# One core, two-layer graph network: where the products of the bias vectors stand, and which engine splits Wv

## The chip, the core and the metric

The kernel runs on one core of one Trainium2 chip. A core has five instruction queues that run side by side and meet only at semaphores: PE (TensorE, matrix products and transposes into PSUM), DVE (VectorE), ACT (ScalarE), POOL (GpSimd) and SP (SyncE, here used to issue DMAs). The metric is the device time of one execution in microseconds; lower is better. Three executions of the kernel before took 311.39 to 311.70 us, median 311.57 us.

## The reference

Node features x (1024 x 512) go through two layers, each on a layer-normed and rectified copy h of x and each added back to x.

```python
def layer_0(h, src, dst):                 # attention over the edges
    q, k, v = h @ Wq + bq, h @ Wk + bk, h @ Wv + bv
    adj = zeros(1024, 1024).at[src, dst].set(1.0)
    a = q @ k.T / sqrt(512)
    a = a * adj + (1.0 - adj) * NEG       # NEG = -1e6
    return softmax(a, axis=-1) @ v

def layer_1(h, src, dst):                 # two rounds of degree-weighted sums over edges plus self loops
    h = agg(h @ W1 + b1)
    h = relu(batch_norm(h) * gamma + beta)
    return agg(h @ W2 + b2)
```

There are 16384 edges, sorted by dst. dst is drawn as 1024 times the square of a uniform number, so low numbers of dst have many more edges than high ones.

## The kernel before, in words

**Products to full precision.** Each f32 operand is split into a rounded part "hi" and the rest "lo", and a product is three matmuls (lines 948 to 950: lo by hi, hi by lo, hi by hi). A tile that PE leaves in PSUM is an *item*: ACT writes its hi (`hi_of`, line 459), then DVE subtracts to get its lo (`lo_of`, line 651). A weight that comes by DMA is split in two loads j = 0, 1 of 128 x 1024 each: before the change ACT copies the hi of Wv (line 414) and DVE makes the lo (line 636).

**Items.** `start` holds 16: the transposes of Wk and Wq (`t`, eight), M = Wq Wk^T in four blocks (`m`), and the transposes of the first four row blocks of h (`h`). `ahead[i]` holds what PE makes ahead of count group i: v = h Wv by row blocks, the other four h, q = h M in quarters, and `w`.

**Count groups.** The edge counts are built in 16 groups of 64 dst each, in the order 14, 15, 0, 1, 2, ... (`ORDER`). For each group DVE writes one-hot tiles chunk by chunk (a chunk is 128 edges): `src_oh` at line 668, one instruction a chunk, and `dst_oh` at line 670, one instruction for a round of two chunks (the first round) or three. PE multiplies them (line 1018), and ends a group with a small matmul (line 1032). A ring of four rounds (`RING`) lies between DVE and PE: DVE can be four rounds ahead. The third group in this order, group 2, is dst 0 to 63, the one with the most edges. The bounds of a group's chunks are read at run time into registers (`bounds_of`, line 660 on DVE).

**Order on DVE, written out by hand.** Early items 0 to 5; one-hots of groups 0 and 1 with items 6 and 7 between; the two lo of Wv (`split_w(0, 0)`, `split_w(0, 1)`); items 8 to 15 (the four `m`, the four `h`); bounds of group 2; then for i = 2 to 15 the lo of `ahead[i - 2]`, the bounds of the next group and the one-hots of group i. After groups 6, 7, 8 and 9 stand the products of the bias vectors with columns of Wk and Wq:

```python
if 6 <= i <= 9:
    columns_of_biases(K if i < 8 else Q, (0, 1) if i % 2 == 0 else (2, 3))
```

Each call multiplies two 128 x 512 blocks by a broadcast bias row and sums along the row into a column of `uw` (line 689); the last call adds bq by bk (line 693). That is nine instructions. Their results are needed by the hi of `q`, from ahead of group 10, and by `w`.

**Order on ACT.** hi of items 0 to 7, `stats(0)` (sums and squares of x blocks 0 and 1), hi of item 8, `split_w(0, (0,))`, `stats(2)`, hi of item 9, `split_w(0, (1,))`, `layer_norm(0..3)` (line 434), hi of items 10 to 15, then the count groups.

**Order on POOL.** Constants; `targets_of(0..2)` (line 355: dst shifted by the group's first, one 128 x 132 instruction a group, which that group's one-hots wait for); `ln1(0)` and `ln1(2)` (lines 349, 314, 351: three small instructions that give the layer norm's factors for x blocks 0, 1 and 2, 3; they wait for the squares from `stats`, and `layer_norm` waits for them); `targets_of(3..7)`, `ln1(4)`, `ln1(6)`, `targets_of(8..15)`.

**Order on PE.** Items 0 to 9, counts of group 0, items 10 and 11, counts of group 1, items 12 to 15 (transposes of h blocks 0 to 3), then for each further group the items of `ahead[i]` and its counts. v block 0 waits for both lo of Wv.

**Order on SP.** Edges, Wq, x blocks 0 to 3, Wv (`load_w(0)`, line 252), x blocks 4 to 7 (each waits for a `layer_norm`, since the four buffers are reused), the bias rows bq and bk into the two places of `bias_row` (line 263, each 2 KB read into 128 partitions), gamma and beta, and more.

Of the kernel before, what the change touches and what calls it, by code (L numbers as in the profile page):

```python
# [17 lines left out]
P = 128  # L18
N = 1024
D = 512  # L20
# [24 lines left out]
ALU = mybir.AluOpType  # L45
ACT = mybir.ActivationFunctionType
AX = mybir.AxisListType
F32 = mybir.dt.float32
# [7 lines left out]
def gnn_kernel(nc, x, src, dst, Wq, bq, Wk, bk, Wv, bv, W1, b1, gamma, beta, W2, b2, out):  # L56
# [61 lines left out]
    bias_row = sb("bias_row", [P, 2, D], F32)  # L118
# [48 lines left out]
    S = {n: ctx.enter_context(nc.semaphore(n)) for n in sem_names}  # L167
# [3 lines left out]
    K, Q = 0, 1  # L171
# [40 lines left out]
    def weight_load(i, j, what):  # L212

        k = KC // LOADS
        w, raw = weights[i][1:3]
        at, part = {"hi": (w, 0), "lo": (w, 1), "raw": (raw, 1)}[what]
        return at[:, part, j * k:(j + 1) * k, :]
# [7 lines left out]
    @block.sync  # L225
    def _(sp):

        sp.dma_start(edge_i[:, 0, :], dst.rearrange("(c j) -> c j", j=P)).then_inc(S["dst_in"], 16)
        sp.dma_start(edge_i[:, 1, :], src.rearrange("(c j) -> c j", j=P)).then_inc(S["src_in"], 16)

        def load_x(n):
            if XT <= n < NT + XT:
                sp.wait_ge(S["h_ready"], n - XT + 1)
            if n >= NT + XT:
                sp.wait_ge(S["x1_ready"], n - NT - XT + 1)
            sp.dma_start(xt[:, n % XT, :], x[(n % NT) * P:(n % NT + 1) * P, :]).then_inc(S[f"x_in{n % XT}"], 16)

        def turn_counts(t):

            if t == 0:  # L240
                sp.wait_ge(S["c16"], 2 * NW)
            if t >= ADJ:
                sp.wait_ge(S["masked"], t - ADJ + 1)
            sp.dma_start_transpose(adj[:, t % ADJ, :].rearrange("p (b n) -> p b n", b=NT),
                                   cnt16[:, t, :, :].rearrange("p b n -> p (b n)")).then_inc(
                S[f"adj_in{t % ADJ}"], 16)

        def load_w(i):

            k = KC // LOADS  # L250
            for j in range(LOADS):
                sp.dma_start(weight_load(i, j, "raw"), weights[i][0].rearrange("(k p) n -> p k n", p=P)[
                    :, j * k:(j + 1) * k, :]).then_inc(S[f"{weights[i][3]}{j}"], 16)

        for j in range(LOADS):
            sp.dma_start(half_of_qk(Q, j), half_in_dram(Wq, j)).then_inc(S[f"Wq_in{j}"], 16)
        for t in range(XT):
            load_x(t)
        load_w(0)
        for t in range(XT, NT):  # L260
            load_x(t)
        for i, b in ((K, bq), (Q, bk)):
            sp.dma_start(bias_row[:, i, :], b.rearrange("(o n) -> o n", o=1).to_broadcast([P, D])).then_inc(S["qk_bias_in"], 16)
        for i, b in enumerate((gamma, beta)):
            sp.dma_start(bcol[:, i, :], b.rearrange("(c p) -> p c", p=P),
                         allow_slow_non_contiguous=True).then_inc(S["bcol_in"], 16)
        for t in range(XT):
            load_x(NT + t)
        sp.wait_ge(S["item_ps"], nth(("v", NT - 1, 0)))
        load_w(1)  # L270
        sp.wait_ge(S["uw_ready"], 4)
        sp.dma_start(bias_row[:, 0, :], bv.rearrange("(o n) -> o n", o=1).to_broadcast([P, D])).then_inc(S["bias_in"], 16)
        sp.dma_start(bias_row[:, 1, :], b1.rearrange("(o n) -> o n", o=1).to_broadcast([P, D])).then_inc(S["b1_in"], 16)
        def turn_p(t, part, split, done, landed):

            sp.wait_ge(S[split], t + 1)
            if t >= 1:
                sp.wait_ge(S[done], t)
            sp.dma_start_transpose(p16T[:, part, :, :], p16[:, part, :]).then_inc(S[landed], 16)

        def turn_h2(t, part, split, done, landed):

            sp.wait_ge(S[split], t + 1)
            if t >= 1:
                sp.wait_ge(S[done], t)
            sp.dma_start_transpose(h16T[:, part, :, :], h16[:, part, :]).then_inc(S[landed], 16)

        for t in range(ADJ):
            turn_counts(t)
        for t in range(NT + 1):  # L290
            if t < NT:
                turn_p(t, 0, "p16_hi", "p_hi", "p16_hi_in")
                turn_p(t, 1, "p16_lo", "p_lo", "p16_lo_in")
            if XT <= t + 3 < NT:
                load_x(NT + t + 3)
            if t == 0:
                load_w(2)
            if t + ADJ < NT:
                turn_counts(t + ADJ)
            if t >= 1:  # L300
                turn_h2(t - 1, 0, "h16_hi", "h2T_hi", "h16_hi_in")
                turn_h2(t - 1, 1, "h16_lo", "h2T_lo", "h16_lo_in")
        sp.wait_ge(S["xb_ready"], NT)
        sp.dma_start(bias_row[:, 0, :], b2.rearrange("(o n) -> o n", o=1).to_broadcast([P, D])).then_inc(S["bias_in"], 16)
        for t in range(NT):
            sp.wait_ge(S["out_ready"], t + 1)
            sp.dma_start(out[t * P:(t + 1) * P, :], xt[:, t % XT, :]).then_inc(S[f"out_done{t % XT}"], 16)
        for u in range(XT):
            sp.wait_ge(S[f"out_done{u}"], 16 * NT // XT)

    @block.gpsimd
    def _(pool):
# [32 lines left out]
        def ln1(t):  # L345

            p = slice(t, t + 2)
            pool.wait_ge(S["x_squares"], t + 2)
            step(pool.tensor_scalar(lnc[:, 1, p], xsum[:, 1, p], 1.0 / D, EPS, ALU.mult, ALU.add))
            step(pw(lnc[:, 2, p], lnc[:, 1, p], 2))  # L350
            pool.tensor_tensor(lnc[:, 3, p], lnc[:, 0, p], lnc[:, 2, p], ALU.mult).then_inc(S["ln_coef"], 2)

        def targets_of(i):

            pool.tensor_scalar(drel(i), dcol[:, :], float(-WIN * ORDER[i]), 0.0, ALU.add, ALU.add).then_inc(S["drel_ready"], 1)

        pool.wait_ge(S["ecol_ready"], 1)
        pool.wait_ge(S["pad_ready"], 1)
        for i in range(3):
            targets_of(i)  # L360
        ln1(0)
        ln1(2)
        for i in range(3, 8):
            targets_of(i)
        ln1(4)
# [40 lines left out]
    def _(act):  # L406
# [3 lines left out]
        def split_w(i, loads=range(LOADS)):  # L410

            for j in loads:
                act.wait_ge(S[f"{weights[i][3]}{j}"], weights[i][4])
                act.activation(weight_load(i, j, "hi"), weight_load(i, j, "raw"),
                               ACT.Copy).then_inc(S["w_hi"], 1)
# [54 lines left out]
            hi_of(item)  # L470
        stats(0)
        hi_of(("m", 0, 0))
        split_w(0, (0,))
        stats(2)
        hi_of(("m", 1, 0))
        split_w(0, (1,))
        for t in range(KC):
            layer_norm(t)
        for item in list(start)[10:]:
# [114 lines left out]
    def _(dve):  # L594
# [39 lines left out]
        def split_w(i, j):  # L634
            dve.wait_ge(S["w_hi"], w_hi_count(i, j))
            dve.tensor_tensor(weight_load(i, j, "lo"), weight_load(i, j, "raw"),
                              weight_load(i, j, "hi").bitcast(F32), ALU.subtract).then_inc(S["w_lo"], 1)
# [21 lines left out]
        def bounds_of(i):  # L659
            return dve.value_load(lohi[0:1, ORDER[i]:ORDER[i] + 1], min_val=256, max_val=257 * NCH)  # L660
# [23 lines left out]
        def columns_of_biases(n, ks):  # L684

            if (n, ks) == (K, (0, 1)):
                dve.wait_ge(S["qk_bias_in"], 32)
            for k in ks:
                ins = dve.scalar_tensor_tensor(out=qk_raw[:, n, k, :], in0=qk_raw[:, n, k, :], scalar=1.0,
                                               in1=bias_row[:, n, :], op0=ALU.mult, op1=ALU.mult,  # L690
                                               accum_out=uw[:, n, k:k + 1])
            if (n, ks) == (Q, (2, 3)):
                ins = dve.scalar_tensor_tensor(out=bias_row[:, 0, :], in0=bias_row[:, 0, :], scalar=1.0,
                                               in1=bias_row[:, 1, :], op0=ALU.mult, op1=ALU.mult, accum_out=bqbk[:, 0:1])
            ins.then_inc(S["uw_ready"], 1)
# [34 lines left out]
        for item in early[6:8]:  # L730
            lo_of(item)
        onehots(1, bounds[1])
        split_w(0, 0)
        split_w(0, 1)
        for item in early[8:]:
            lo_of(item)
        bounds = bounds_of(2)
        for i in range(2, NW):
            for item in ahead[i - 2]:
                lo_of(item)  # L740
            now = bounds
            if i + 1 < NW:
                bounds = bounds_of(i + 1)
            onehots(i, now)
            if 6 <= i <= 9:
                columns_of_biases(K if i < 8 else Q, (0, 1) if i % 2 == 0 else (2, 3))
        for i in range(NW - 2, NW):
            for item in ahead[i]:
                lo_of(item)
# [480 lines left out]
```

## Time and profile before

| | |
|---|---|
| timed executions | 311.39, 311.57, 311.70 us |
| profiled execution, first to last instruction (span) | 309.8 us |
| median of the timed executions less that span | 1.77 us |
| PE busy | 295.1 us, 95% |
| DVE busy | 210.2 us, 68% |
| ACT busy | 143.6 us, 46% |
| POOL busy | 55.4 us, 18% |
| granted TensorE clock, mean | 0.999 |

The profile lists no time of its own for the profiled execution beside its span; what lies around the span is taken as 1.77 us. A busy time is an average over stages: the change touches the stretch from 4 to about 100 us, where the edge counts are built. A line of the timeline gives the start, the time of a run of like instructions, the engine, the line of the kernel, the operation and, in brackets, how long the engine sat idle before and what ended that. Instructions of one engine can overlap at their ends, so the pace of a run is taken from start to start.

### The profile page before, as it was taken

Reading aid. Unit: us, or ns where it says so; the run is one execution under the profiler, and the core shown is the slowest. Engines: PE = TensorE matmul, PEld = TensorE weight load, DVE = VectorE, ACT = ScalarE, POOL = GpSimd, SP = SyncE. Lnnn points to the kernel's source line nnn. Section 1 sums busy time; section 2 is a strip of 40 time slices with the busy share of each in tenths; the row PEclk is TensorE's granted clock in tenths of the full one; section 3 lists DMA queues with packets and bytes.
Section 4 is the critical chain, followed back from the end, with each engine's and each line's share of the span. In section 5 each row is a group of like instructions: output and inputs, shape, how many; then the busy total and the mean of one; then the engine's idle time right before and its main releaser. Section 6 shows DMA issues by size and latency. Waiting matters only on the chain.

```text
span 309.8 us, 4740 instructions
## 1 busy us (share of the span) xinstructions
PE 295.1 (95%) x1319; PEld 227.4 (73%) x1319; DVE 210.2 (68%) x470; ACT 143.6 (46%) x245; POOL 55.4 (18%) x96
## 2 busy tenths in 40 slices
PE   2999969899999999999999999999999999999995
PEld 2977436565666688888888888888788888888884
DVE  3787999999997747667647575757444288376311
ACT  1799944443445626635465445437632035233000
POOL 5234280000000170032121212203010043100000
PEclk9999999999999999999999999999999999999999
DMA  7707040000420127832834636133203000000221
GB/s 268 291 3 204 1 135 0 3 0 0 150 57 3 33 36 107 200 85 53 136 69 102 135 46 124 36 68 59 44 0 70 1 0 2 0 0 2 101 103 68
DMA packets 42310, 21.65 MB, mean 70 GB/s; under 512 B 35760, under 2 KB 36016, under 8 KB 42288
## 3 DMA queue, kind: packets, MB, share of 16 engines
q1 hardware_dynamic: 41744, 20.33, 26.9%
q10 hardware_dynamic: 544, 1.05, 0.9%
q8 instruction: 11, 0.18, 0.2%
q14 instruction: 11, 0.09, 0.1%
HBM read 10.88 MB, written 2.10 MB: 42 GB/s over the span
## 4 chain that ended last, share of the span: by engine, by line
PE 79%; DVE 10%; issue 4%; DVEq 4%; DMA 1%; ACT 1%; SPq 0%; ACTq 0%
PE ps L948 18%; PE ps L950 18%; PE ps L949 18%; PE ps L1196 9%; PE ps L1119 8%; PE ps L1018 5%; DVE src_oh L668 4%; PE ps L986 2%; DVEq L668 2%; DVE dst_oh L670 2%; DMA edge_i<-src_in 1%; DVE hT L651 1%; DVEq L670 1%; DVEq L660 0%; DVEq L674 0%
## 5 line engine op out<-in xcount | busy, mean ns | idle before, releaser
L668 DVE TENSOR_SCALAR src_oh<-iota,ecol 128x512 f16 x149 | 44.2, 346 | 4.0 <-issue 2.9
L1018 PE MATMUL ps<-src_oh,dst_oh 128*128 x149 | 37.9, 382 | 5.4 <-DVE dst_oh L670 4.6
L1018 PEld LDWEIGHTS ps<-src_oh,dst_oh 128*128 x149 | 14.4, 103 | 25.6 <-issue 16.7
L1119 PE MATMUL ps<-cnt,qh 128*128 128x512 f32 x128 | 30.1, 391 | 0.3 <-ACT cnt L541 0.3
L1196 PE MATMUL ps<-qh,cnt 128*128 128x512 f32 x128 | 29.3, 390 | 0.0
L443 ACT ACTIVATE cnt<-ps 64x512 int16<-64x512 f32 x32 | 18.9, 592 | 20.7 <-PE ps L1032 20.3
L1119 PEld LDWEIGHTS ps<-cnt,qh 128*128 128x128 f32 x128 | 23.9, 188 | 5.6 <-DVE qh L827 0.7
L1196 PEld LDWEIGHTS ps<-qh,cnt 128*128 128x128 f32 x128 | 23.9, 188 | 5.2 <-DVE vb L929 0.3
L950 PE MATMUL ps<-v,pT 128*128 128x512 f32 x64 | 25.0, 390 | 0.0
L948 PE MATMUL ps<-v,pT 128*128 128x512 f32 x64 | 24.9, 390 | 0.0
L949 PE MATMUL ps<-v,pT 128*128 128x512 f32 x64 | 24.9, 390 | 0.0
L948 PE MATMUL ps<-hT,qh 128*128 128x512 f32 x64 | 24.9, 389 | 0.0
L949 PE MATMUL ps<-hT,qh 128*128 128x512 f32 x64 | 24.9, 389 | 0.0
L950 PE MATMUL ps<-hT,qh 128*128 128x512 f32 x64 | 24.9, 389 | 0.0
L382 POOL TENSOR_SCALAR lnb<-bnag 128x1 f32<-128x1 f32 x8 | 8.2, 1028 | 82.2 <-DVE bnag L801 82.2
L941 DVE SCALAR_TENSOR_TENSOR xt<-ps,dinv,x 128x512 f32<-128x512 f32 x8 | 5.7, 747 | 17.1 <-PE ps L1196 17.1
L790 DVE TENSOR_SCALAR pT<-p16T 128x1024 fp32r<-128x1024 f16 x8 | 5.5, 693 | 15.9 <-DMA p16T<-p 15.8
L768 DVE COPY_PREDICATED T<-adj,ps 128x1024 f32<-128x1024 int16 x8 | 10.6, 1322 | 7.8 <-PE ps L950 7.8
L525 ACT ACTIVATE hnT<-h16T 128x512 fp32r<-128x512 f16 x8 | 5.1, 632 | 23.2 <-DMA h16T<-h 23.2
L497 ACT ACTIVATE T<-T,smx 128x1024 f32<-128x1024 f32 x8 | 9.2, 1150 | 13.1 <-DVE smx L773 13.1
L466 ACT ACTIVATE T<-zerob,fill 128x1024 f32<-128x1024 bf16 x8 | 9.1, 1147 | 11.9 <-DVE p L780 11.9
L670 DVE TENSOR_TENSOR dst_oh<-iota_w,drel_first 128x384 f16 (+1 forms) x35 | 14.4, 411 | 0.0
(176 smaller groups left out, 658.8 us busy)
## 6 DMA issues: line engine op xcount, KB each, us to landing
xt<-x_in SPq DMA_DIRECT2D x16, 256.0 KB, 3.3
out<-xt SPq DMA_DIRECT2D x8, 256.0 KB, 2.1
qk_raw<-L_gnn_Wk_in ACTq DMA_DIRECT2D x2, 512.0 KB, 4.9
qk_raw<-L_gnn_Wq_in SPq DMA_DIRECT2D x2, 512.0 KB, 6.7
wB_raw<-L_gnn_Wv_in SPq DMA_DIRECT2D x2, 512.0 KB, 8.9
wB_raw<-L_gnn_W_in SPq DMA_DIRECT2D x2, 512.0 KB, 4.3
w_raw<-L_gnn_W_in SPq DMA_DIRECT2D x2, 512.0 KB, 4.8
bias_row<-L_gnn_b_in SPq DMA_DIRECT2D x2, 256.0 KB, 3.7
```

What stands on the lines that cost most here:

```text
L443: act.activation(cnt16[rows, a * KC:(a + 1) * KC, w // 2, :], ps[a * WIN:(a + 1) * WIN, i % 2, :].rearrange("p (s n) -> p s n", n=P), ACT. ...
L466: act.activation(T[:, t % 2, :], zerob[:, 0:1].to_broadcast([P, N]), ACT.Identity, bias=fill[:, t:t + 1]).then_inc(S["mask_set"], 1)
L497: act.activation(T[:, t % 2, :], T[:, t % 2, :], ACT.Exp, bias=smx[:, 1, t:t + 1], scale=SCALE, accum_out=smx[:, 2, t:t + 1]).then_inc(S[" ...
L668: dve.tensor_scalar(src_oh[:, bass.ds(slot, 1), j, :].rearrange("p a n -> p (a n)"), iota[:, :], ecol[:, bass.ds(c + j, 1)], None, ALU.is_ ...
L670: dve.tensor_tensor(dst_oh[:, bass.ds(slot, 1), :, 0:count].rearrange("p a n u -> p (a n) u"), iota_w[:, :, 0:count], drel(i)[:, bass.ds(c ...
L768: dve.copy_predicated(T[:, t % 2, :], adj[:, t % ADJ, :], ps[:, 2 * (t % 2):2 * (t % 2) + 2, :].rearrange("p a n -> p (a n)")).then_inc(S[ ...
L948: pe.matmul(out_, stat(1), mov(0), start=first, stop=False)
L949: pe.matmul(out_, stat(0), mov(1), start=False, stop=False)
L950: return pe.matmul(out_, stat(0), mov(0), start=False, stop=last)
L1018: m = pe.matmul(ps[:, i % 2, :], dst_oh[:, bass.ds(slot, 1), :, j].rearrange("p a n -> p (a n)"), src_oh[:, bass.ds(slot, 1), j, :].rearra ...
L1119: m = pe.matmul(bank(g), qh[:, d, a, c * P:(c + 1) * P], cnt[:, d, n * HALF:(n + 1) * HALF], start=(d == 0 and a == 1), stop=last)
L1196: m = pe.matmul(bank(t), cnt[:, d, t * P:(t + 1) * P], qh[:, d, a, :], start=(d == 0 and a == 1), stop=last)
```

## The change

SP issues the two bias rows right behind Wv, ahead of the waits for x blocks 4 to 7. The split of Wv goes from ACT and DVE to POOL, between `targets_of` and the layer norm's factors. On DVE the two lo of Wv are gone; the four products of Wk's columns stand between the lo of items 8 and 9, and the five of Wq's columns (with bq by bk) behind the bounds of group 2, ahead of that group's one-hots. Nothing stands behind groups 6 to 9 any more.

```diff
         load_w(0)
+        for i, b in ((K, bq), (Q, bk)):
+            sp.dma_start(bias_row[:, i, :], b.rearrange("(o n) -> o n", o=1).to_broadcast([P, D])).then_inc(S["qk_bias_in"], 16)
         for t in range(XT, NT):
             load_x(t)
-        for i, b in ((K, bq), (Q, bk)):
-            sp.dma_start(bias_row[:, i, :], b.rearrange("(o n) -> o n", o=1).to_broadcast([P, D])).then_inc(S["qk_bias_in"], 16)
...
+        def wv_hi(j):
+
+            pool.wait_ge(S[f"wB_in{j}"], 16)
+            pool.tensor_copy(weight_load(0, j, "hi"), weight_load(0, j, "raw")).then_inc(S["w_hi"], 1)
+
+        def wv_lo(j):
+
+            pool.wait_ge(S["w_hi"], w_hi_count(0, j))
+            pool.tensor_tensor(weight_load(0, j, "lo"), weight_load(0, j, "raw"),
+                               weight_load(0, j, "hi").bitcast(F32), ALU.subtract).then_inc(S["w_lo"], 1)
+
         for i in range(3):
             targets_of(i)
+        wv_hi(0)
         ln1(0)
+        wv_hi(1)
+        wv_lo(0)
         ln1(2)
+        wv_lo(1)
         for i in range(3, 8):
             targets_of(i)
...
         stats(0)
         hi_of(("m", 0, 0))
-        split_w(0, (0,))
         stats(2)
         hi_of(("m", 1, 0))
-        split_w(0, (1,))
...
         onehots(1, bounds[1])
-        split_w(0, 0)
-        split_w(0, 1)
-        for item in early[8:]:
+        lo_of(early[8])
+        columns_of_biases(K, (0, 1))
+        columns_of_biases(K, (2, 3))
+        for item in early[9:]:
             lo_of(item)
         bounds = bounds_of(2)
+        columns_of_biases(Q, (0, 1))
+        columns_of_biases(Q, (2, 3))
         for i in range(2, NW):
             for item in ahead[i - 2]:
                 lo_of(item)
...
             onehots(i, now)
-            if 6 <= i <= 9:
-                columns_of_biases(K if i < 8 else Q, (0, 1) if i % 2 == 0 else (2, 3))
```

## Rows read from the trace of the kernel before

**Rows 1.** Busy time by stretch: length, then us busy of each engine, clock, DMA
```profile
18.40:26.40 8.00, 8.00 (x39) 5.70 (x39) 5.67 (x12) 7.88 (x17) 4.65 (x8) 1.00 0.22 62
...
30.80:45.90 15.10, 12.09 (x51) 5.96 (x50) 15.03 (x51) 10.81 (x28) 8.21 (x14) 1.00 0.23 70
```

**Rows 2.** PE's waits from 33 to 46 us: us in total, times, longest
```profile
PE ps L1018 <- DVE dst_oh L670: 2.8, 7, 0.5
```

**Rows 3.** The chain that ended last, 26 to 31.5 us: start, us, what
```profile
26.89 0.61 ACT hT L459
...
27.52 2.06 DVE hT L651 x4
...
29.68 0.31 DVEq L660
...
30.03 0.20 DVEq L660
...
30.79 0.12 DVE src_oh L668
```

**Rows 4.** Timeline of PE, start of count group 2; groups 6, 7, 8 and 10
```profile
33.86 2.56 PE L1018 MATMUL ps<-src_oh,dst_oh 128*128 x11
...
65.91 1.91 PE L1018 MATMUL ps<-src_oh,dst_oh 128*128 x8
67.65 0.18 PE L1032 MATMUL ps<-zerob 128*128 128x32 bf16 x1
...
70.52 1.28 PE L1018 MATMUL ps<-src_oh,dst_oh 128*128 x5
...
72.77 0.18 PE L1032 MATMUL ps<-zerob 128*128 128x32 bf16 x1
...
75.63 2.15 PE L1018 MATMUL ps<-src_oh,dst_oh 128*128 x8
77.62 0.18 PE L1032 MATMUL ps<-zerob 128*128 128x32 bf16 x1
...
85.52 0.61 PE L1018 MATMUL ps<-src_oh,dst_oh 128*128 x2
...
86.97 0.18 PE L1032 MATMUL ps<-zerob 128*128 128x32 bf16 x1
```

**Rows 5.** Timeline of DVE, the three products behind group 9
```profile
81.55 0.67 DVE L689 SCALAR_TENSOR_TENSOR qk_raw<-qk_raw,bias_row 128x512 f32<-128x512 f32 x1
...
83.39 0.67 DVE L651 TENSOR_TENSOR v<-ps,v 128x512 fp32r<-128x512 f32 x1
```

**Rows 6.** Timeline of all engines, 16 to 26 us
```profile
16.94 0.19 POOL L349 TENSOR_SCALAR lnc<-xsum 128x2 f32<-128x2 f32 x1 [4.81 <-ACT T L428]
...
18.09 0.20 POOL L351 TENSOR_TENSOR lnc<-lnc 128x2 f32<-128x2 f32 x1
...
20.10 1.22 DVE L636 TENSOR_TENSOR wB<-wB_raw,wB 128x1024 fp32r<-128x1024 f32 x1
...
22.69 2.92 ACT L434 ACTIVATE T<-xt,lnc 128x512 f32<-128x512 f32 x4
...
22.82 1.28 DVE L636 TENSOR_TENSOR wB<-wB_raw,wB 128x1024 fp32r<-128x1024 f32 x1 [1.50 <-ACT wB L414]
...
25.52 1.06 ACT L459 ACTIVATE M<-ps 128x512 fp32r<-128x512 f32 x2
```

**Rows 7.** DMA issues of the page: KB each, us to landing
```profile
wB_raw<-L_gnn_Wv_in SPq DMA_DIRECT2D x2, 512.0 KB, 8.9
...
bias_row<-L_gnn_bk_in SPq DMA_DIRECT2D x1, 256.0 KB, 4.7
```

**Rows 8.** POOL's groups by line and shape: busy, mean ns
```profile
L378 POOL TENSOR_TENSOR xt<-xt,bias_row 128x512 f32<-128x512 f32 x8 | 10.2, 1293 | 10.7 <-DMA xt<-x_in 10.7
...
L335 POOL CAST identb<-ident 128x128 bf16<-128x128 f32 x1 | 0.3, 291 | 0.0
```

**Rows 9.** Line 355 on POOL, 22 to 27 us: ns min/median/max
```profile
L355 POOL TENSOR_SCALAR drel_first<-dcol x5: 650/656/1250, 22.7 to 25.9; 128x132 f16<-128x132 f16 x5
```

## The prediction

> **What bounds the kernel now.** The page's shares (table above) say only that PE leads and that DVE may bind in places. So I cut the stretch that the edit touches into stages. In count group 2, from 30.8 to 45.9 us, DVE is busy 15.03 of 15.10 us and PE 12.09 [rows 1]; PE's waits there are for `dst_oh`, 2.8 us in seven pieces [rows 2]. So in this group DVE's one-hots set the pace, and whatever delays their start delays the end of the group by as much: the reader should see that DVE has no idle time to absorb anything. Ahead of it, from 18.4 to 26.4, it is the other way round: PE is busy 8.00 of 8.00 us and DVE 5.67 [rows 1]. Between the two lies a handover that the chain of waits spells out: ACT's hi of h block 0 from 26.89, the four lo of h on DVE from 27.52, two register loads, and the first one-hot at 30.79 [rows 3]. From group 6 on PE leads again: its eight chunks take 67.65 - 65.91 = 1.74 us without a wait [rows 4].
>
> **The change, part by part.**
>
> *Products of Wk's columns, four, moved from groups 6 and 7 to 20 us.* Three products take 83.39 - 81.55 = 1.84 us, start to start, so 0.613 us each [rows 5]; four are 2.45 us. The two lo of Wv that leave the same place took 1.22 and 1.28 us with an idle gap of 1.50 between them [rows 6], 4.0 us. DVE is free of one-hots at 20.10; lo of item 8 (0.6) and the four products end near 23.2, item 9 near 23.8. Items 10 and 11 can't come before ACT's hi of them, which started at 25.52 [rows 6]. Cost: nothing, with about 2 us of cover. The bias rows must have landed by 20.7: Wv took 8.9 us from an issue near 5 us, so to about 14, and a bias row took 4.7 us [rows 7]; even one behind the other that is 19. Cost nothing; without this cover DVE would stand until they land, at most as long as they are late.
>
> *Products of Wq's columns, five, moved from groups 8 and 9 to the handover.* 5 x 0.613 = 3.07 us, on the path: they stand behind the lo of h block 3 and ahead of the first one-hot of the group in which DVE sets the pace. They hide something. At the same pace DVE ended the four lo near 27.52 + 4 x 0.613 = 29.97 and started the one-hot at 30.79: 0.81 us in which only registers were loaded and worked out [rows 3]. The first load (29.68 to 29.99) now lies ahead of the products and under the last lo; the second and the arithmetic behind it (30.03 to 30.79) come behind the products, and the queue can begin them while the last product runs, as it began the first load before the last lo had ended. How much is left bare no row shows: between 0 and 0.81. I take 0.4, the middle: the nearest row is the first load, which was covered, but it is a third of this work. Delay of the first one-hot: 3.07 + 0.4 - 0.81 = 2.66 us, from 2.26 to 3.07. Group 2 then ends as much later, and PE and everything behind it with it; the next groups' one-hots and v blocks keep their distances.
>
> *What comes back.* From group 6 on PE leads and DVE's lateness shows only as stretched count groups. Eight chunks unhindered: 1.74 us. Group 7: 72.77 - 70.52 = 2.25, so 0.51 lost. Group 8: 77.62 - 75.63 = 1.99, 0.25 lost; group 9 has the same form (80.54 to 82.56), 0.28 lost. Group 10 has five chunks, 1.09 by the same pace, and took 86.97 - 85.52 = 1.45: 0.36 lost [rows 4]. These are the groups behind the calls in question, and each call is 1.2 to 1.8 us of DVE; without them DVE is ahead by more than these losses. Back: 0.51 + 0.25 + 0.28 + 0.36 = 1.40 us; bounds 0 (PE finds another wait) and 1.40.
>
> *Wv's split on POOL.* ACT loses two copies; that only lets `stats(2)` end near 20.2. POOL's work is new, and no row shows it at this size. The lo (two inputs, 1024 columns) by the row of 512 columns, 1.29 us, less a fixed 0.19 (line 349, two columns): 0.19 + 2 x 1.10 = 2.4 us; twice the whole row is 2.6 [rows 6, 8]. The hi copy by the cast of 128 columns, 0.29: 0.19 + 8 x 0.10 = 1.0 us as I take it, 2.3 if eight times the whole row; the far end, the 128 x 132 f16 row of 0.65 scaled, is 5.0 [rows 8, 9]. What waits behind: `ln1(2)`, and behind that on ACT layer norms 2 and 3, the hi of items 10 and 11, and the hi of h block 0, which is in the chain. wv_hi(0) runs from about 14 to 15, ahead of `ln1(0)` at 16.94, which ends at 18.29 [rows 6]. Then wv_hi(1) to 19.4. Then wv_lo(0): 1.3 us of it are done by 20.7, when DVE starts Wk's products. Beside a DVE instruction that reads two SBUF operands POOL slows: one `targets_of` took 1.25 us beside line 636 on DVE, against 0.65, and DVE's own 1.28 against 1.22 [rows 6, 9]. At that pace of 0.52 the last 1.1 us take 2.1, to 22.9. `ln1(2)` takes 1.35, as `ln1(0)` did (16.94 to 18.29), with a little drag, to 24.4. Layer norms 2 and 3 end at 24.4 + 2 x 0.73 = 25.9, items 10 and 11 at 26.9, h block 0 at 27.5. That is where it ended before (26.89 + 0.61). So the POOL path has used up its slack to the last tenth, and every excess is passed on. I add 0.2 us; bounds 0 and, with the copy at 2.3 us, 1.2; with the far end of 5.0, about 3.8. wv_lo(1) ends near 27, ahead of v block 0, which can't start before the lo of h block 0 (from 27.52 [rows 3]).
>
> The Trainium skill (SBUF — State Buffer, "Who interferes with whom") has a rule against this: a DVE instruction with two SBUF inputs and a GpSimd instruction that reads SBUF exclude each other, and the second to issue blocks fully until the first ends. The row above bears out POOL's loss (0.60 us) but not a loss for DVE (0.06 us). By the rule the sum would be that of the second rival.
>
> *Moves at no cost.* `targets_of(3..7)` starts near 27 instead of 22.73; group 3 needs them after 45. x blocks 4 to 7 are loaded a little earlier. SP issues two DMAs more ahead of waits of many us.
>
> **Sum.** 2.66 + 0.2 - 1.40 = +1.46 us on the span of 309.8 us, so 311.3. The profiled execution has no other time of its own; with the 1.77 us around the span that the median of 311.57 implies, the median should become 313.0 us.
>
> **Rivals.**
>
> *The group's start hides the products.* PE enters group 2 only after v blocks 0 and 1, at 33.86 [rows 4], 3 us after DVE began its first one-hot; with four rounds of ring, DVE's delay could vanish if PE were the later of the two at the end of the group. Then only the give-back is left: -1.40 us, 310.2. It decides the case if PE does not wait for one-hots late in group 2. Against it: the seven waits, up to 0.5 us, and DVE busy for 15.03 of 15.10 us. For it: nothing but the start of the group. The sign also turns wherever the delay falls below 1.40.
>
> *The shared port locks.* wv_lo(0) and Wk's products exclude each other. If POOL holds first, the products run from 22 to 24.5, `ln1(2)`'s steps each wait for one of them, and h block 0 is about 1.2 us late. If DVE holds first, wv_lo(0) starts at 23.2: 25.6 its end, 27.0 `ln1(2)`, 28.4 the layer norms, 30.1 the hi of h block 0, 2.6 late. Sum 2.66 - 1.40 + 1.2 to 2.6 = +2.5 to +3.9: 314.0 to 315.4, say 314.6. For it: the doubled `targets_of`. Against: DVE's 0.06.
>
> *Nothing comes back.* PE's losses in groups 7 to 10 stay, from some handshake rather than DVE's lateness: 2.66 + 0.2 = +2.9, 314.4. Against: group 6, with the same form of handshake, shows no loss.
>
> **Chances.** Forecast 0.63 (its own range 312.3 to 314.0), lock 0.18, nothing back 0.11, hidden 0.08. What this kernel's measurement can tell from no change is 0.2%, 0.62 us. Faster by more: the hidden case less a part of it, 0.07. Within: the rest of that and the forecast's low tail, 0.08. Slower: 0.85. The range, with the low end of the delay below and the POOL bounds and the lock above: 312.0 to 315.0.
>
> **What would show it.** Right: first one-hot of group 2 near 33.6; PE's waits in group 2 as before but about 2.7 us later; groups 7 to 10 at 1.74 and 1.09 us; POOL's lo near 2.4 us, more beside Wk's products; h block 0's hi within half a microsecond of 26.89. Wrong: group 2 ending near 45.9 (products hidden); h block 0 late by over 1 us (lock, or a slow copy); groups 7 to 10 still stretched.

## The result, and the profile after

The changed kernel takes 314.76 us, median of four executions (314.49 to 315.43), against 311.48 us (311.33 to 311.70, four) for the kernel before on the same chip: ratio 1.0111, 95% interval 1.0098 to 1.0124. It is slower by 3.28 us; the forecast was +1.46. The profiled execution took 314.49 us with a span of 312.7 us, 2.9 more than before.

Read first what DVE does ahead of group 2. Its timeline in the kernel after (one-hots now lines 681 and 683, products 702 and 706, lo 664):

```profile
17.37 1.38 DVE L681 TENSOR_SCALAR src_oh<-iota,ecol 128x512 f16 x2
18.67 2.62 DVE L683 TENSOR_TENSOR dst_oh<-iota_w,drel_first 128x256 f16 x1
21.21 0.87 DVE L681 TENSOR_SCALAR src_oh<-iota,ecol 128x512 f16 x3
...
22.34 0.68 DVE L664 TENSOR_TENSOR M<-ps,M 128x512 fp32r<-128x512 f32 x1
22.94 2.45 DVE L702 SCALAR_TENSOR_TENSOR qk_raw<-qk_raw,bias_row 128x512 f32<-128x512 f32 x1
...
25.32 0.77 DVE L702 SCALAR_TENSOR_TENSOR qk_raw<-qk_raw,bias_row 128x512 f32<-128x512 f32 x1
...
27.41 1.88 DVE L664 TENSOR_TENSOR M<-ps,M 128x512 fp32r<-128x512 f32 x3
29.21 2.47 DVE L664 TENSOR_TENSOR hT<-ps,hT 128x512 fp32r<-128x512 f32 x4
31.61 0.68 DVE L702 SCALAR_TENSOR_TENSOR qk_raw<-qk_raw,bias_row 128x512 f32<-128x512 f32 x1
...
34.66 0.61 DVE L681 TENSOR_SCALAR src_oh<-iota,ecol 128x512 f16 x2
```

and POOL's, with its hi (line 362) and lo (line 367) of Wv:

```profile
17.40 1.20 POOL L362 CAST wB<-wB_raw 128x1024 fp32r<-128x1024 f32 x1
18.57 2.44 POOL L367 TENSOR_TENSOR wB<-wB_raw,wB 128x1024 fp32r<-128x1024 f32 x1
...
22.27 0.20 POOL L351 TENSOR_TENSOR lnc<-lnc 128x2 f32<-128x2 f32 x1
22.43 2.41 POOL L367 TENSOR_TENSOR wB<-wB_raw,wB 128x1024 fp32r<-128x1024 f32 x1
24.80 3.93 POOL L355 TENSOR_SCALAR drel_first<-dcol 128x132 f16<-128x132 f16 x5
```

Lay the two side by side. "Alone" means the time that the same instruction takes with POOL idle. A `dst_oh` that takes 0.42 us started 0.10 us behind POOL's first lo and took 2.62: it ended 0.28 us behind that lo. A product, 0.68 us alone, started 0.51 us behind the second lo and took 2.45, to 0.55 us behind its end. The other three products take 0.77 beside `targets_of`, only 0.09 more than alone, and the pair of `src_oh` beside POOL's hi 1.38 instead of 0.61. DVE's account, start to start: group 1's one-hots 17.37 to 22.34, 4.97 us, where the kernel before took 18.12 to 20.10, 1.98; four products 22.94 to 27.41, 4.47 us instead of the 2.45 reckoned. That is 5.0 us lost beside POOL (0.27 of it the 3 x 0.09 beside `targets_of`). Without it DVE's work from group 1 to the lo of h would have been 1.98 + 0.60 + 2.45 + 1.80 (three lo of M) = 6.83 us, and the kernel before took 27.52 - 18.12 = 9.40 [rows 3]: 2.57 us of cover, that is, of idle time which this work, the products included, would leave. 5.01 - 2.57 = 2.44 us stay. The lo of h starts only 1.69 us later, because this execution was 0.75 us ahead by then (17.37 against 18.12).

The stretches that answer to [rows 1], with group 2 now from 34.66 to 49.60:

```profile
18.40:26.40 8.00, 8.00 (x41) 5.91 (x40) 8.00 (x12) 5.59 (x11) 7.69 (x8) 1.00 0.43 133
34.66:49.60 14.94, 11.67 (x48) 5.47 (x47) 14.94 (x53) 7.64 (x19) 7.93 (x14) 1.00 0.22 71
```

In the first one DVE's 5.67 us of 8.00 have become 8.00 (an instruction that is held counts as busy): the idle time that was to hide the products is gone. Group 2 itself is as before, DVE busy throughout, and PE's wait that answers to [rows 2] has 3.1 us in eight pieces:

```profile
PE ps L1032 <- DVE dst_oh L683: 3.1, 8, 0.5
```

The chain of waits, 26 to 35.5 us, no longer goes through ACT's hi of h as in [rows 3] but straight back through DVE's products:

```profile
25.40 2.10 DVE qk_raw L702 x6
27.49 1.80 DVE M L664 x3
```

PE, with the rows that answer to [rows 4] (two idle gaps ahead of v block 0; start and end of group 2; groups 7 and 10):

```profile
28.15 0.66 PE L1000 MATMUL ps<-ident,T 128*128 128x128 f32 x4 [0.85 <-DVE M L664]
29.99 0.47 PE L962 MATMUL ps<-wB,hT 128*128 128x512 f32 x1 [1.18 <-DVE hT L664]
...
37.12 2.87 PE L1032 MATMUL ps<-src_oh,dst_oh 128*128 x11
...
49.57 0.18 PE L1046 MATMUL ps<-zerob 128*128 128x32 bf16 x1
...
74.65 1.91 PE L1032 MATMUL ps<-src_oh,dst_oh 128*128 x8
76.39 0.18 PE L1046 MATMUL ps<-zerob 128*128 128x32 bf16 x1
...
88.47 1.26 PE L1032 MATMUL ps<-src_oh,dst_oh 128*128 x5
89.56 0.18 PE L1046 MATMUL ps<-zerob 128*128 128x32 bf16 x1
```

Group by group PE ends later than before by 3.70 us (group 2: 45.87 to 49.57), 4.15 (group 5: 63.01 to 67.16), 3.62 (group 7), 2.59 (group 10: 86.97 to 89.56) and 2.50 (group 15: 104.11 to 106.61). The rest of the 2.9, about 0.4 us, is added much later, at 250 us, and is taken up below.

### The profile page after: what moved, and what is told of

Same layout as the page of the kernel before. It is cut to its first block, busy times and chain, and to the rows that moved or that the text cites. A ratio compares the mean times of both kernels' runs of the same rounds, so it can differ in the third digit from the quotient of the medians.

```text
span 312.7 us, 4740 instructions
## 1 busy us (share of the span) xinstructions
PE 295.8 (95%) x1319; PEld 227.6 (73%) x1319; DVE 213.2 (68%) x468; ACT 141.8 (45%) x243; POOL 62.2 (20%) x100
## 4 chain that ended last, share of the span: by engine, by line
PE 71%; DVE 16%; issue 5%; DVEq 4%; ACT 2%; DMA 1%; POOL 0%; SPq 0%; ACTq 0%; POOLq 0%
PE ps L962 17%; PE ps L964 17%; PE ps L963 16%; PE ps L1210 9%; PE ps L1133 6%; PE ps L1032 5%; DVE src_oh L681 4%; DVE dst_oh L683 3%; DVEq L681 2%; DVE qk_raw L702 2%; DMA edge_i<-src_in 1%; DVE WT L664 1%; DVE M L664 1%; PE ps L1000 1%; DVE bnst L931 1%
## 5 line engine op out<-in xcount | busy, mean ns | idle before, releaser
L681 DVE TENSOR_SCALAR src_oh<-iota,ecol 128x512 f16 x149 | 45.4, 357 | 6.2 <-PE ps L1032 4.0
L683 DVE TENSOR_TENSOR dst_oh<-iota_w,drel_first 128x384 f16 (+1 forms) x35 | 16.6, 474 | 0.0
L962 PE MATMUL ps<-wB,hT 128*128 128x512 f32 x32 | 13.7, 428 | 1.2 <-DVE hT L664 1.2
```

Source lines behind the costliest of these rows:

```text
L681: dve.tensor_scalar(src_oh[:, bass.ds(slot, 1), j, :].rearrange("p a n -> p (a n)"), iota[:, :], ecol[:, bass.ds(c + j, 1)], None, ALU.is_ ...
L683: dve.tensor_tensor(dst_oh[:, bass.ds(slot, 1), :, 0:count].rearrange("p a n u -> p (a n) u"), iota_w[:, :, 0:count], drel(i)[:, bass.ds(c ...
L962: pe.matmul(out_, stat(1), mov(0), start=first, stop=False)
```

## The experiments

Each is compared with runs of the kernel before on its own chip. Three explanations are weighed here. The lock: POOL's lo and DVE's instruction exclude each other for whole instructions, and that eats the cover of Wk's products. The products: the excess is the products themselves (the bare registers, or nothing given back). The clock: PE ran slowly. A numbered or lettered theory in the text ahead of a run belongs to that run alone.

**One half at a time (e1, e2).** Only POOL's split:

```diff
+        for item in early[8:]:                      # the order of before, without split_w(0, ...)
+            lo_of(item)
...
+            if 6 <= i <= 9:
+                columns_of_biases(K if i < 8 else Q, (0, 1) if i % 2 == 0 else (2, 3))
```

> POOL splits Wv as in the changed kernel; the nine products stay behind groups 6 to 9 as before. Theory 1 (port: a POOL instruction that reads SBUF and a DVE instruction that reads two SBUF operands or runs in a fast mode hold each other up): group 1's one-hots on DVE take about 5 us instead of 2.0, one dst_oh near 2.6 us beside POOL's first lo; DVE still has cover until the lo of h block 0, so the time stays near 311.5 (311.0 to 312.0). Theory 2 (placement: the products' place alone made the loss, POOL is innocent): dst_oh stays at 0.42 us, group 1's one-hots at 2.0 us; time 311.5 too. The instruction times tell them apart, not the total.

311.96 us against 311.61, ratio 1.0013 (1.0003 to 1.0022). The hold is there, on other instructions: the `dst_oh` that was to be held kept its 0.42 us (18.66 to 19.08), and the second `src_oh` of the next round took 2.50 (from 20.05, 0.10 us behind POOL's lo) instead of 0.35. POOL's hi came 0.09 us behind a `src_oh` here, did not hold it, and itself took 1.49 instead of 1.04. DVE:

```profile
19.00 3.81 DVE L681 TENSOR_SCALAR src_oh<-iota,ecol 128x512 f16 x3
...
27.59 2.48 DVE L664 TENSOR_TENSOR hT<-ps,hT 128x512 fp32r<-128x512 f32 x4 [0.18 <-ACT hT L474]
```

and POOL:

```profile
18.49 1.49 POOL L362 CAST wB<-wB_raw 128x1024 fp32r<-128x1024 f32 x1
19.95 2.44 POOL L367 TENSOR_TENSOR wB<-wB_raw,wB 128x1024 fp32r<-128x1024 f32 x1
```

Group 1's one-hots took 4.92 us here too, 2.94 too many, yet the lo of h begins at 27.59 against 27.52: without the products the same cover swallows the hold.

Only the products moved (Wv split by ACT and DVE as before, Wk's products between the two lo of Wv):

```diff
+        lo_of(early[8])
         split_w(0, 0)
+        columns_of_biases(K, (0, 1))
+        columns_of_biases(K, (2, 3))
         split_w(0, 1)
-        for item in early[8:]:
+        for item in early[9:]:
...
+        columns_of_biases(Q, (0, 1))
+        columns_of_biases(Q, (2, 3))
```

> All nine products moved as in the changed kernel, bias rows early, but Wv is split by ACT and DVE as before (on DVE: lo of item 8, first lo of Wv, Wk's products, second lo of Wv). Theory 1: no long one-hot, each product 0.61 us, first lo of h at 27.5 (less about 0.9 if the early part runs ahead as in the changed kernel's profile), the first one-hot of group 2 2.2 us later than before, 1.6 us given back in groups 7 to 10: 312.1 (311.8 to 312.6). Theory 2: the changed kernel's time, 314.5 or more.

312.63 us, ratio 1.0033 (1.0021 to 1.0044), +1.02, just above the expected 311.8 to 312.6. No product is long, the lo of h begins at 27.62, and the first one-hot stands at the end of the last product:

```profile
32.45 0.69 DVE L693 SCALAR_TENSOR_TENSOR bias_row<-bias_row 128x512 f32<-128x512 f32 x1
33.07 0.62 DVE L668 TENSOR_SCALAR src_oh<-iota,ecol 128x512 f16 x2
```

Group 2 ends 2.12 us late, group 10 1.01 us late. So the forecast's sum for the products (2.66 - 1.40 = 1.26) was near. The two halves make 0.35 + 1.02 = 1.4 us apart and 3.28 together: they use one cover twice. That speaks against the products alone, and it is what the lock needs.

**Wq's products back behind groups 8 and 9 (e3)**, the rest as changed:

```diff
-        columns_of_biases(Q, (0, 1))
-        columns_of_biases(Q, (2, 3))
...
+            if 8 <= i <= 9:
+                columns_of_biases(Q, (0, 1) if i == 8 else (2, 3))
```

> The changed kernel, but Wq's products go back behind groups 8 and 9. Theory 1: DVE still loses about 5 us beside POOL, the lo of h start 1.7 us late, the first one-hot of group 2 follows 1.2 us behind the last lo of h; groups 7 and 8 give back, 9 and 10 little: 312.9 (312.3 to 313.4). Theory 2: the delay was Wq's products, so the time falls to 311.0 to 311.6.

313.14 us, ratio 1.0042 (1.0028 to 1.0057). The first one-hot stands at 31.87, 2.79 us earlier than in the changed kernel, but group 2 ends only 0.48 earlier, at 49.09. Between them PE's v blocks 0 and 1 run at half the clock and DVE, its ring full, waits for them. The waits from 30 to 50 us, then the stretches (length, busy times in the order of [rows 1], clock):

```profile
DVE src_oh L681 <- PE ps L1032: 2.2, 1, 2.2
```

```profile
28.00:30.00 2.00, 0.65 (x4) 0.42 (x4) 2.00 (x4) 1.36 (x3) 0.92 (x2) 1.00 0.00 0
...
32.00:34.00 2.00, 2.00 (x7) 1.51 (x6) 2.00 (x8) 1.89 (x7) 0.00 (x0) 0.50 0.00 0
```

So the clock costs time here, as a second consequence of the late lo of h: PE stood 0.69 and 1.19 us, then ran slowly. The ten executions bear it out: five with a mean granted clock of 0.993 to 0.995 took 313.40 to 313.78 us, the five with 0.999 or 1.000 took 311.89 to 312.87. The median of 313.14 lies between the two groups, so that it met the expected range is partly luck. In the changed kernel the same clock (0.50 from 31 to 33 us) shows no price: DVE did not wait there and PE waits for `dst_oh` again from 40 us, and in the two runs of that kernel the four executions with 0.995 took 314.49 to 314.67 us, the four with 0.998 or 1.000 took 314.86 to 315.43.

**POOL's lo in four pieces (e5):**

```diff
+            for a in range(2):
+                for h in range(2):
+                    at = slice(h * D // 2, (h + 1) * D // 2)
+                    ins = pool.tensor_tensor(weight_load(0, j, "lo")[:, a, at], weight_load(0, j, "raw")[:, a, at],
+                                             weight_load(0, j, "hi")[:, a, at].bitcast(F32), ALU.subtract)
+            ins.then_inc(S["w_lo"], 1)
```

> The changed kernel, with each of POOL's two lo instructions cut into four of 128 x 256. Theory 1a (whoever comes first holds the port for its whole instruction): a POOL piece takes about 0.7 us, so no DVE instruction is held up by more than about that: the longest dst_oh 1.2 us instead of 2.62, the longest of Wk's products 1.4 us instead of 2.45; the pieces alternate with DVE's instructions, so DVE's loss in sum stays at 3 to 5 us and the time at 314.0 to 315.0. Theory 1b (the two share a rate): DVE instructions beside POOL all take about twice their time, none over 1.3 us, also in the changed kernel. That kernel's 2.62 already speaks against 1b; the pieces test whether the length of the hold follows the length of POOL's instruction.

313.74 us against 311.70, ratio 1.0071 (1.0055 to 1.0087): 1.24 us of the 3.28 are gone. A DVE instruction is now held for one piece at most, and POOL is held in its turn. DVE's loss is 3.8 us (group 1's one-hots 17.44 to 22.20, the products 22.80 to 26.30) instead of 5.0, within the expected 3 to 5; the time lies below the expected 314.0 to 315.0. DVE:

```profile
18.75 0.95 DVE L687 TENSOR_TENSOR dst_oh<-iota_w,drel_first 128x256 f16 x1
...
22.80 0.68 DVE L706 SCALAR_TENSOR_TENSOR qk_raw<-qk_raw,bias_row 128x512 f32<-128x512 f32 x1
...
24.02 1.22 DVE L706 SCALAR_TENSOR_TENSOR qk_raw<-qk_raw,bias_row 128x512 f32<-128x512 f32 x1
```

POOL's second four pieces took 4.17 us instead of 2.41. The lo of h starts at 28.10 instead of 29.21.

**POOL that only writes (e6)**, a constant by iota in place of its hi, and of its lo likewise, so that this kernel leaves out the split of Wv:

```diff
-            pool.tensor_copy(weight_load(0, j, "hi"), weight_load(0, j, "raw")).then_inc(S["w_hi"], 1)
+            pool.iota(weight_load(0, j, "hi"), pattern=[[0, 2], [0, D]], base=1, channel_multiplier=0,
+                      allow_small_or_imprecise_dtypes=True).then_inc(S["w_hi"], 1)
```

> The changed kernel, with Wv's split left out: POOL writes a constant into the places of hi and lo (iota, 128 x 1024, no SBUF input) instead of reading Wv. Theory A (the read side alone is contended): no product and no dst_oh is held up (0.61 and 0.42 us); src_oh may be. Theory B (any POOL instruction holds DVE up): the DVE instruction that starts beside an iota is held up by about 1 us. Under A the lo of h start at 27.5 and the time is near 312.2 to 312.8, as with the products alone moved; under B 313 to 314.

312.77 us, ratio 1.0036 (1.0021 to 1.0051). Group 10 ends at 87.95, as with the products alone (87.98). DVE, then POOL:

```profile
17.91 1.38 DVE L680 TENSOR_SCALAR src_oh<-iota,ecol 128x512 f16 x2
19.21 0.41 DVE L682 TENSOR_TENSOR dst_oh<-iota_w,drel_first 128x256 f16 x1
19.54 1.34 DVE L680 TENSOR_SCALAR src_oh<-iota,ecol 128x512 f16 x3
...
21.75 0.68 DVE L701 SCALAR_TENSOR_TENSOR qk_raw<-qk_raw,bias_row 128x512 f32<-128x512 f32 x1
```

```profile
18.02 1.13 POOL L362 IOTA wB<- 128x1024 fp32r x1
19.11 1.08 POOL L367 IOTA wB<- 128x1024 fp32r x1
...
21.54 0.99 POOL L367 IOTA wB<- 128x1024 fp32r x1
```

The products and `dst_oh`, with two inputs each, run at full pace beside a POOL instruction that reads nothing (the product at 21.75 lies within the iota that began at 21.54); `src_oh`, with one f16 input, is held all the same. This separates reading from the mere presence of POOL: the part of the loss that hung on the lo's reads is gone. (An iota is also shorter, 1.08 us for 2.44, so the two causes of a smaller loss come together for `src_oh`, not for the products, which were not held at all.)

**The changed kernel once more (e10):**

> The changed kernel once more, on the same chip as e9. If GpSimd's lower half and VectorE's instruction hold each other for their whole length in every execution, a one-hot of destinations takes about 2.6 us and the first product of Wk's rows about 2.4 us again, the lower halves of h begin 1.5 us or more later than the 27.5 us of the kernel before, and the time is 314.4 to 315.2 us. If the hold is a matter of which instruction happens to come first, at least one of the two is short (under 1 us) in this execution, and the time lies 1 us or more below.

314.77 us (314.66 to 315.36) against 311.61, ratio 1.0108 (1.0093 to 1.0124). The same two instructions are held, `dst_oh` 2.61 us and the first product 2.44, and the lo of h starts at 29.16. The two are held in both profiles of this kernel, and in e3's as well (2.61 and 2.44), so it is not a chance meeting.

**Towards a better version (e4, e7, e8, e9).** In e4 Wv is split by ACT and DVE, Wk's products stand between its two lo and Wq's behind groups 7 and 9:

```diff
         split_w(0, 0)
+        columns_of_biases(K, (0, 1))
+        columns_of_biases(K, (2, 3))
         split_w(0, 1)
...
-            if 6 <= i <= 9:
-                columns_of_biases(K if i < 8 else Q, (0, 1) if i % 2 == 0 else (2, 3))
+            if i in (7, 9):
+                columns_of_biases(Q, (0, 1) if i == 7 else (2, 3))
```

> Wv split by ACT and DVE as before; Wk's products stand between the two lo of Wv ahead of group 2, Wq's behind groups 7 and 9. Theory 1: no lock, Wk's products are covered by DVE's idle time before the lo of h, Wq's fit where PE leads: groups 7 to 10 lose 0.3 us or less instead of 1.4; 310.3 (310.0 to 310.9). Theory 2: Wk's products ahead of group 2 are not covered, the lo of h start 1 to 2 us late: 311.5 to 312.5.

310.05 us, ratio 0.9952 (0.9939 to 0.9966). Here Wk's products really are covered (lo of h at 27.27), and the time falls by 1.5 us.

e7 is the same with all `targets_of` ahead of `ln1(4)`:

```diff
-        for i in range(3, 8):
+        for i in range(3, NW):
             targets_of(i)
         ln1(4)
         ln1(6)
-        for i in range(8, NW):
-            targets_of(i)
```

> The kernel with Wk's products in the gap and Wq's behind groups 7 and 9, and targets_of(8..15) moved on POOL from behind ln1(6) to behind targets_of(7), so beside the lo of h (one operand in PSUM) instead of beside four rounds of group 2's one-hots. Theory 1: those rounds fall from 1.29 to 1.15 us, group 2 ends 0.5 us earlier: 309.5 (309.2 to 309.9). Rival: the 1.29 has another cause (ACT or the rounds themselves), no change against 310.05.

309.65 us, ratio 0.9935 (0.9921 to 0.9948). The late rounds of group 2 take 1.13 us instead of 1.29, since POOL's targets no longer read beside them, but the first one-hot now waits 0.62 us for a target; group 2 ends 0.31 us earlier, where 0.5 was expected. The intervals of the two overlap, so the times do not show a gain over e4's kernel.

e8 has the register loads of groups 2 and 3 also ahead of the lo of h:

```diff
-        for item in early[9:]:
+        for item in early[9:12]:
+            lo_of(item)
+        bounds = [bounds_of(2), bounds_of(3)]
+        for item in early[12:]:
             lo_of(item)
```

> As the run before, and the bounds of groups 2 and 3 are loaded ahead of the four lo of h instead of behind them. If the 0.76 us without work ahead of group 2's first one-hot are the two register loads and the arithmetic in about equal parts, the loads' 0.3 to 0.4 us go: 309.2 (308.8 to 309.6). Rival: the queue loads them no earlier or PE's arrival at group 2 sets its end: no change against the run before.

309.21 us, ratio 0.9920 (0.9905 to 0.9935). The first one-hot follows the last lo without the 0.76 us of idle time that e4's kernel still shows there. Yet group 2's matmuls end at 45.31, as with e7's kernel (45.29): the lo of h began later in this execution (27.89 against 27.46), the first one-hot stood only 0.26 us earlier (30.29 against 30.55), and behind the group DVE waits for PE (0.4 us there, 0.6 here). The intervals of the two times overlap. The time met its range, but group 2's end, through which the gain would have to come, did not move, so the rival of no change is not excluded.

Last, e9, the targets spread ahead of and between the layer norms:

```diff
-        for i in range(3):
+        for i in range(8):
             targets_of(i)
         ln1(0)
+        for i in range(8, 12):
+            targets_of(i)
         ln1(2)
-        for i in range(3, NW):
+        for i in range(12, NW):
             targets_of(i)
```

> The kernel of e8 with the other targets moved too: those of column groups 0 to 7 ahead of the layer norm of blocks 0 and 1, 8 to 11 between it and that of blocks 2 and 3, 12 to 15 behind it; no target instruction of GpSimd then runs beside VectorE's one-hots of group 2. If the first rounds of group 2 are long because GpSimd's target products read beside them, group 2's one-hot rounds take about 1.15 us from the first on, group 2's matmuls end 0.3 to 0.4 us earlier than e8's, and the time is about 308.8 us (308.4 to 309.2). The rival: GpSimd's small products now run beside the one-hots of groups 0 and 1 and ahead of the layer norm, which comes later by their 16 instructions; if h block 0 is late for it, the first one-hot of group 2 stands 0.5 us or more later than e8's 30.3 us and the time is 309.2 us or above.

309.03 us (308.58 to 309.62) against 311.61, ratio 0.9918 (0.9903 to 0.9933). The time lies in the expected range, the reason for it does not hold: the second and third rounds do take 1.11 and 1.13 us, but then DVE's ring is full and DVE waits 0.57 us for PE (and 0.62 ahead of the next group), and from PE's first matmul of group 2 to its end it is 11.08 us in both kernels (33.89 to 44.97; 34.23 to 45.31). The 0.34 us by which the group ends earlier was there at its start, and 0.30 of it at the first one-hot of all (14.23 against 14.53). What the one-hots gain ahead of PE's entry into the group is lost at the full ring; behind it DVE's rounds, 1.15 us each, still set the pace, since PE waits 2.3 us for `dst_oh` in both kernels. The last two kernels are the fastest, 2.5 and 2.6 us under the kernel before, and not to be told apart.

## Why the prediction missed

**The step that failed** is the cost of Wk's products: "Cost: nothing, with about 2 us of cover", and under it DVE's own loss beside POOL, taken as 0.06 us ("DVE's own 1.28 against 1.22"). The cover was sized well (2.57 us by the account above). It had room for the products, but not for the 5.0 us that DVE lost beside POOL as well: 2.44 us of them were left over. Undoing POOL's reads (e6) brings group 10 from 89.56 to 87.95, and leaving POOL out (e2) to 87.98, so the hold costs 1.6 us there. In spans the whole is 0.9 (the products alone, e2: 310.7 against 309.8) + 1.6 (the hold) + 0.4 (a late wait, last section) = 2.9 us.

**How the row was misread.** [rows 9] gives one `targets_of` of 1.25 us. I read a doubled time as a lower pace and DVE's 1.28 as proof that DVE does not suffer. The place of these instructions in the trace of before says otherwise. Two `targets_of` met that lo:

```profile
22.73 0.67 POOL L355 TENSOR_SCALAR drel_first<-dcol 128x132 f16<-128x132 f16 x1
...
23.37 1.25 POOL L355 TENSOR_SCALAR drel_first<-dcol 128x132 f16<-128x132 f16 x1
```

DVE's lo ran from 22.82 to 24.10. The second `targets_of` came 0.55 us behind its start and ended 0.52 us behind its end, at 24.62, as if it had stood still until then: POOL was held, not slowed. The first began 0.09 us ahead of the lo, and DVE still lost no more than 0.06. So this POOL instruction costs DVE little even where it comes first, and the row could not say what a lo of 2.4 us would do. In the changed kernel POOL comes first by 0.10 and 0.51 us, with instructions of 2.4 us, and DVE stands to their end. The same products beside `targets_of` (last row of POOL's timeline above) lost 0.09 each, while POOL's instructions there took:

```profile
L355 POOL TENSOR_SCALAR drel_first<-dcol x5: 654/727/1111, 24.8 to 28.1; 128x132 f16<-128x132 f16 x5
```

Had the two excluded each other for whole instructions, a product and a `targets_of` would take at least 0.61 + 0.65 us; they went at 0.70 a pair. Why this instruction holds DVE for so much less than its recorded length is not shown. The products alone (e2) show POOL held again: with DVE first, POOL's two-column instruction of 0.19 us takes 1.07:

```profile
21.43 1.07 POOL L349 TENSOR_SCALAR lnc<-xsum 128x2 f32<-128x2 f32 x1 [2.99 <-ACT T L428]
```

The Trainium skill (SBUF — State Buffer, "Who interferes with whom") has this rule: the shared port pair is locked for a whole instruction, and issue order decides who blocks; a DVE instruction with two SBUF inputs meets only GpSimd instructions that read, one in a two-port mode meets any. The traces agree for POOL's lo, hi and iota: 2.62 and 2.45 us behind a lo, 0.41 and 0.68 beside an iota, while `src_oh` is held by the hi and by the iota (1.38 for the pair); that `src_oh` runs in a two-port mode no trace shows. They do not agree for `targets_of`, which reads SBUF and did not hold the products for its whole length. I had given that rival 0.18, and asked of the row the wrong thing: it had to be read by who came first and by what POOL's instruction was, not only by whose time grew.

**The lock rival**, at 314.6 us, was nearest to the measured 314.76, but in part by luck. It put h block 0 1.2 to 2.6 us late; its hi came on time and its lo 1.69 late, 2.44 with this execution's lead taken out. It named the wrong victims in part: it let the products and `ln1(2)` suffer, and left out group 1's one-hots, which lost 3.0 of the 5.0 us. I had wv_lo(0) begin at 19.4; it began at 18.57, beside them, and the product that was held stood behind wv_lo(1).

**Wq's products** cost what they were to: 5 x 0.61 = 3.05 us between the last lo and the first one-hot (31.61 to 34.66), and no register time is left bare (0.4 was taken, 0 was the lower bound). The delay from this part is 3.05 - 0.82 = 2.23 instead of 2.66. Together with 1.69, less 0.05 (the four lo were that much quicker), it is the 3.87 us by which the first one-hot is late (30.79 to 34.66).

**Give-back**: group 7 now takes 76.39 - 74.65 = 1.74 (groups 8 and 9 the same) and group 10 89.56 - 88.47 = 1.09, as forecast. From its peak of 4.15 us behind group 5 the lateness falls to 2.49 by group 11: 1.66 came back, 1.40 was forecast. "Nothing comes back" is refuted.

**POOL's sizes** were right: lo 2.44 and 2.41 us (2.4), hi 1.04 and 1.20 (1.0). POOL's path was not late: `ln1(2)` ended at 22.47, not 24.4, h block 0's hi came at 26.46, and the 0.2 us added for it was not needed. DVE, not POOL, paid for the meeting.

**Hidden** (group 2 at 45.9) is refuted: 49.57.

**A term that I had not thought of** is 0.4 us at 250 us; see the last section.

## What to carry to other kernels

When an instruction is long because of a neighbour on GpSimd or VectorE, look up which of the two started first: DVE stood behind a lo of 2.4 us to its end, and POOL stood behind DVE where DVE came first. A doubled time on one engine and none on the other is no proof that the other is safe. What an instruction costs its neighbour need not be its whole length (0.09 us beside `targets_of`), so price the very instruction that is to move, not another one. Before giving GpSimd work to relieve VectorE, list VectorE's instructions in that stretch by their inputs: here 4.85 us of lo, 1.2 of hi and the targets behind them took 5.0 us from VectorE, to relieve it of 2.5 [rows 6]. And two edits that are each covered by the same idle time must be priced together: 0.35 and 1.02 us apart, 3.28 together.

## What the runs showed that was not expected

**A late wait that follows who splits Wv.** In the first aggregation (line 914 before, 928 after) DVE's second `g` waits for PE in one case and hardly at all in the other. Before:

```profile
247.71 0.69 DVE L914 TENSOR_TENSOR g<-ps,T 128x512 f32<-128x512 f32 x1 [0.24 <-DVE bnst L917]
```

After:

```profile
250.54 0.69 DVE L928 TENSOR_TENSOR g<-ps,T 128x512 f32<-128x512 f32 x1 [0.59 <-PE ps L1133]
```

The 0.59 stands in all six profiles of kernels in which POOL writes Wv's halves (the changed one twice, e1, e3, e5, e6), the 0.23 or 0.24 in all six of the others (before, e2, e4, e7 to e9). From the first `g` to the end of the span it is 64.1 to 64.3 us in those (248.52 to 312.7 in the changed kernel) and 63.7 to 63.9 in these (246.05 to 309.8 before). It accounts for about 0.4 of the 3.28 us, and for the 0.35 of e1's kernel, where group 15 ends 0.10 us late only. Nothing in this stretch uses Wv, and PE's matmuls keep their pace of 0.23 us. The cause is not shown.

**The clock behind two short gaps.** In the changed kernel PE sat idle for 0.85 us and then, with 0.66 us of transposes between, for 1.18. The granted clock of PE's stretches (length, PE busy, clock):

```profile
29.00:30.00 1.00, 0.01 (x1) 1.00 0.00 0
30.00:31.00 1.00, 1.00 (x4) 0.74 0.00 0
31.00:32.00 1.00, 1.00 (x4) 0.50 0.00 0
...
34.00:35.00 1.00, 1.00 (x6) 1.00 0.02 8
```

It fell from 2.4 to 1.2 GHz when PE was busy again, and v's matmuls stand 0.43 us apart instead of 0.23. With only the second of the gaps (e5: 1.18 us) the clock stayed at 1.00.

**A lead early on.** The first one-hot of all came at 14.03 and 14.05 us in the two profiles of the changed kernel and between 13.90 and 14.95 in those of the others, before any instruction that the edits touch on DVE; it makes single times of this stretch uncertain by up to a microsecond. Its cause is open.
